# Two loads held back, a clock filler moved, an earlier gather and later landing times in the planned orders of a recommendation-model kernel

## What is computed

```
sparse_embed = emb_tables[field_idx[None, :], x_sparse]
gram = jnp.einsum('bik,bjk->bij', sparse_embed, sparse_embed)
inner = gram[:, iu, ju]
dnn_in = jnp.concatenate([x_dense, z, inner], axis=-1)
h = jax.nn.relu(dnn_in @ w1 + b1)
out = jax.nn.sigmoid(h @ w2 + b2)
```

## Time and profile before

| what | value |
|---|---|
| median of 3 runs | 213.66 us (212.72 to 214.28) |
| profiled execution, its own time | 214.66 us |
| its span, first to last instruction | 212.5 us |
| TensorE busy | 201.6 us (95%) |
| VectorE, ScalarE, GpSimd busy | 148.6, 129.3, 129.4 us |
| mean granted TensorE clock | 0.992 of full speed |

### The profile page before, as it was taken

How to read it: one execution, slowest core, us unless ns; L and a number is a source line. 1 busy time by engine, 2 the same in 40 slices (tenths; PEclk the granted TensorE clock), 3 DMA queues, 4 the chain that set the end, 5 groups by cost and what they waited for, 6 DMA issues and landing times.

```text
span 212.5 us, 3900 instructions
## 1 busy us (share of the span) xinstructions
PE 201.6 (95%) x1340; PEld 161.4 (76%) x1340; DVE 148.6 (70%) x347; ACT 129.3 (61%) x256; POOL 129.4 (61%) x210
## 2 busy tenths in 40 slices
PE   8859999999999999999999799799999999999994
PEld 8834888877777878776887688588888877788882
DVE  3559457488937779879459796777587679773483
ACT  2657443479948939977338844679698558542201
POOL 4887888888787878218877878788788500000000
PEclk9997999999999999999999999999999999999999
DMA  5676999968484912326965667698975637223100
GB/s 153 188 226 201 305 327 344 323 203 281 119 291 125 299 51 63 86 56 169 325 217 178 196 180 189 185 329 299 325 213 161 207 98 212 87 35 63 32 0 0
DMA packets 15388, 39.00 MB, mean 184 GB/s; under 512 B 3881, under 2 KB 5281, under 8 KB 15369
## 3 DMA queue, kind: packets, MB, share of 16 engines
q1 hardware_dynamic: 11688, 35.27, 51.3%
q0 software_dynamic: 3328, 3.41, 7.6%
q10 hardware_dynamic: 353, 0.08, 0.2%
HBM read 37.71 MB, written 0.69 MB: 181 GB/s over the span
## 4 chain that ended last, share of the span: by engine, by line
PE 69%; POOL 15%; DMA 6%; issue 5%; DVE 3%; ACT 2%; DVEq 0%; POOLq 0%; ACTq 0%
PE slot L1079 20%; PE slot L1082 19%; PE slot L1085 19%; POOL E L823 13%; DMA E<-emb,row_idx 5%; PE slot L1039 4%; PE slot L1018 3%; POOL pace L831 2%; DVE G L977 2%; PE slot L1071 1%; PE slot L1069 1%; PE slot L1070 1%; ACT w_hi L847 1%; DMA x_idx<-idx 1%; DVE slot L1003 1%
## 5 line engine op out<-in xcount | busy, mean ns | idle before, releaser
L823 POOL DMA_INDIRECT E<-emb,row_idx x104 | 111.7, 1074 | 37.8 <-POOL pace L831 25.7
L929 DVE TENSOR_TENSOR w_lo<-w_raw,w_hi 128x500 fp32r<-128x500 f32 (+6 forms) x128 | 80.8, 671 | 13.2 <-ACT w_hi L847 12.5
L847 ACT CAST w_hi<-w_raw 128x1000 fp32r<-128x1000 f32 (+6 forms) x64 | 65.7, 1029 | 27.3 <-DMA w_raw<-w 15.4
L1079 PE MATMUL slot<-w_hi,x_hi 128*128 128x500 f32 (+5 forms) x236 | 75.0, 399 | 3.4 <-ACT x_hi L873 2.1
L1082 PE MATMUL slot<-w_lo,x_hi 128*128 128x500 f32 (+5 forms) x236 | 73.3, 390 | 2.3 <-DVE w_lo L929 2.2
L1085 PE MATMUL slot<-w_hi,x_lo 128*128 128x500 f32 (+5 forms) x236 | 72.7, 389 | 0.0
L1079 PEld LDWEIGHTS slot<-w_hi,x_hi 128*128 128x128 f32 (+2 forms) x236 | 43.0, 189 | 15.3 <-ACT x_hi L873 5.0
L1082 PEld LDWEIGHTS slot<-w_lo,x_hi 128*128 128x128 f32 (+2 forms) x236 | 44.5, 189 | 12.1 <-DVE w_lo L929 3.0
L1085 PEld LDWEIGHTS slot<-w_hi,x_lo 128*128 128x128 f32 (+2 forms) x236 | 44.4, 189 | 9.3 <-DVE x_lo L959 0.2
L878 ACT COPY ET<-T 32x128 f32<-32x128 f32 (+4 forms) x88 | 32.1, 364 | 2.0
L946 DVE STREAM_TRANSPOSE T<-E 128x256 f32<-128x256 f32 x24 | 10.6, 443 | 18.8 <-DMA E<-emb,row_idx 18.6
(11 more groups left out here) (39 smaller groups left out, 85.8 us busy)
## 6 DMA issues: line engine op xcount, KB each, us to landing
w_raw<-w SPq DMA_DIRECT2D x32, 501.0 KB, 4.7
w_raw<-w SPq DMA_DIRECT2D x32, 500.0 KB, 4.7
E<-emb,row_idx POOLq DMA_INDIRECT x104, 4.3
w_all<-w SPq DMA_DIRECT2D x1, 1001.0 KB, 6.9
gram_dram<-G SPq DMA_DIRECT2D x8, 84.5 KB
x_in<-gram_dram SPq DMA_DIRECT2D x8, 42.0 KB
x_in<-G SPq DMA_DIRECT2D x4, 58.5 KB
x_in<-G SPq DMA_DIRECT2D x4, 19.5 KB
```

What stands on the lines that cost most here:

```text
L823: nc.gpsimd.indirect_dma_start(out=E[:, k % ER, j, :], out_offset=None, in_=emb_rows, in_offset=bass.IndirectOffsetOnAxis(ap=row_idx[:, at ...
L847: nc.scalar.copy(w_parts(m)[0], w_source(m)).then_inc(w_hi_ready, 1)
L929: nc.vector.tensor_tensor(lo[:, cols], w_source(m)[:, cols], hi[:, cols].bitcast(F32), ALU.subtract)\
L1079: nc.tensor.matmul(acc[q], xh, hi[:, cols[q]], start=first, stop=False)
```

## The change

Four edits. (1) Loads 2 and 3 wait for arrival 1 instead of arrival 0. (2) The five filler matmuls stand ahead of product 3 instead of product 2, and write to the accumulator of the product that follows them. (3) Arrival 16 waits for two gram rounds, and arrival 17 for four. (4) The planner takes landings as 1.5, 2.0, 1.9, 1.9 us for arrivals 0 to 3 and 3.1 us for all later ones, and knows the new waits; all four lists of orders come out of it anew.

```diff
-KEEP_AT, KEEP = 2, 5
+KEEP_AT, KEEP = 3, 5
-PAUSE, RESUME = 16, 4
+HELD_BACK = {16: 2, 17: 4}
+LAND = (1.5, 2.0, 1.9, 1.9, 3.1)
@@ make_orders, gather
-            if k == PAUSE:
-                if ("gram", RESUME - 1) not in done:
+            if k in HELD_BACK:
+                if ("gram", HELD_BACK[k] - 1) not in done:
                     return
-                pool_at = max(pool_at, done["gram", RESUME - 1] + HOP)
+                pool_at = max(pool_at, done["gram", HELD_BACK[k] - 1] + HOP)
             for _ in range(GROUP_GATHERS[ARRIVALS[k][1]]):
                 pool_at += 1.25 if k < 2 else 1.50
                 g_issued.append(pool_at)
-            e_landed.append(pool_at + (1.3 if k < 2 else 1.9))
+            e_landed.append(pool_at + LAND[min(k, len(LAND) - 1)])
@@ make_orders, update
                 if m < BEHIND:
-                    at = e_landed[0]
+                    at = e_landed[1]
@@ build, sync
                     if EARLY <= m < BEHIND:
-                        sp.wait_ge(e_landed[0], 16 * GROUP_GATHERS[ARRIVALS[0][1]])
+                        sp.wait_ge(e_landed[1], 16 * GROUP_GATHERS[ARRIVALS[1][1]])
@@ build, gpsimd
-                if k == PAUSE:
-                    pool.wait_ge(gram_done, RESUME)
+                if k in HELD_BACK:
+                    pool.wait_ge(gram_done, HELD_BACK[k])
@@ build, tensor
-                        nc.tensor.matmul(slot[SLOT[1, 1, "all"]][:, 0:BANK].rearrange("p (a b) -> p a b", a=4), ones[:],
+                        nc.tensor.matmul(slot[SLOT[cell_at(step)]][:, 0:BANK].rearrange("p (a b) -> p a b", a=4), ones[:],
```

## The result

The changed kernel takes 211.81 us in the median of 22 runs, the kernel before 213.65 us in as many beside it. The ratio is 0.9917 with a 95% interval of 0.9895 to 0.9938: 1.8 us, between 1.3 and 2.2, are gained. 211.0 was forecast. A ratio leaves out each kernel's slow runs, those more than 1.5% above its fastest one, so it can differ a little from the ratio of the medians, which are of all runs. The profiled execution took 211.75 us, with a span of 209.4 us where the kernel before had 212.5. These two spans lie 3.1 us apart, more than the medians: the profile before had its clock fall at the start, and it lies 1.0 us above its median.

The account below looks back on a forecast made before the run. TensorE, 95% busy, was taken as the bound, in phase A together with POOL's chain of gathers. Terms -0.15 - 1.42 - 1.09 - 0.35 + 0.3 = -2.7 us took the median from 213.66 to 211.0 us; range 209.2 to 214.6.

Parts of the forecast that it names:

- Start: Loads 2 and 3 and filler: TensorE 3.7 us ahead at product 4, lead mostly lost to later gathers; valued at 0.15 us.
- The predicted 19.6 for product 4: Product 4 starts at 19.6 instead of 23.37, when x_hi of arrival 2 ends.
- What swallows it: Phase A: arrival 4's landing lets 2.5 us of lead pass; gathers at 1.39 us and more apiece wear it off.
- the 62 that was said to be fixed: Product 32, first to need arrival 9's x_hi, was to start again at 62; well before 61.5 would show otherwise.
- Arrival 16: Its gathers go out from 87, everything behind arrival 17 comes 6.3 us earlier; phase B stalls go, less a small cost.
- the 1.42 us: TensorE's idle time ahead of product 78, behind arrival 21's landing, goes: -1.42 us.
- the 0.35 us: Product 66's loss on a low split in VectorE's queue goes: -0.35 us.
- the 1.09 us: TensorE's idle time at 118.27, product 67 waiting for x_hi of (bt 3, group 6), goes: -1.09 us.
- The 0.3 us for the store and fetch: Cost of four gathers flying during the first store and fetch, which feeds inner products: 0.3 us, between 0 and 1.5.
- The orders: New lists from later planned landings: taken as 0; bounds 0.5 us gain and 1.4 us loss per misplaced x_hi.
- Rival D: ScalarE's list, arrivals 4 to 27: x_hi behind a w_hi waiting for TensorE's release of a piece; 216.6 us; chance 0.12.
- Rival C: Phase B stalls only exchanged as new lists place x24 or x_hi elsewhere; 0.5 us left, 213.2 us; chance 0.28.

Follow-up runs that it names:

- filler8: The changed kernel with eight filler matmuls instead of five: 211.51 us, 0.9889 of the kernel before.
- no_filler: The changed kernel without the five filler matmuls: 211.89 us, 0.9928 of the kernel before.
- start_only: The kernel before with only loads 2 and 3 waiting for arrival 1 and the filler ahead of product 3, old lists: 0.9997 of the kernel before.
- no_pace: The changed kernel with POOL's pacing memset and wait only up to the twelfth gather, so denser gathers: 210.45 us, 0.9819 of the kernel before.
- swap_one: The changed kernel with x_hi of (bt 3, group 6) moved ahead of piece 38's w_hi in ScalarE's list: 212.54 us, 0.9879 of the kernel before.
- g16_start: The kernel before with the change's POOL waits, load waits and filler place, old lists with two entries moved: 211.05 us, 0.9877 of the kernel before.
- g16_nopace: The kernel before with the change's POOL waits and pacing only up to the twelfth gather, old lists: 209.69 us, 0.9837 of the kernel before.

## Why the prediction was right, and where it was off

**Start.** Right where it counts. The predicted 19.6 for product 4 was 19.4, the filler's 4.3 was 4.45, the landing of 3.0 was 3.1. The 19.6 was in part luck: it was to be the end of the x_hi of arrival 2, but that was written from 17.86, and TensorE reached product 4 without waiting, at the end of its own work. That the lead would be lost was predicted with 0.15 us left; 0.36 is left at 98.42 in the pair of profiles, and two experiments moved product 4 by 2.2 us one way (filler8) and 1.0 us the other (no_filler) and the end by less than 1 us. That product 1 passes without a stop whatever VectorE's order held in start_only too. Wrong without the new lists was the sentence behind it, that x_hi of arrival 1 is ready by about 11.9: in start_only ScalarE's list put it behind a w_hi that waited for load 2, and it came at 14.64. I had looked at VectorE's list alone.

**What swallows it.** I named the pace of POOL's gathers. The runs bear this out in part only. That TensorE stands still for the landings of arrivals 4 and 5 is shown, and so is that arrival 4, issued 0.7 us earlier, did not land earlier. Product 32 started at 61.51, half a microsecond before the 62 that was said to be fixed. With denser gathers (no_pace) no landing from arrival 6 to 16 was waited for, and the inner products began no earlier than in the changed kernel; so the pace is not all that holds this stretch, and what does is not separated. Beside this: the Trainium skill (DMA: Bandwidth & Descriptors, Anatomy of one DMA) gives a DMA that GpSimd issues 2.0 us plus its bytes at 436 GB/s, an estimated 2.1 us for a gather. The traces do not agree: the gathers issued between 20 and 31 us in the changed kernel took 5.2 us in the median, and the quickest of the whole run 2.4.

**Arrival 16.** The term was -1.42 - 1.09 - 0.35 + 0.3 = -2.56 us. In the pair of profiles phase B gave 2.7 us, which is the sum but not the terms: the 1.42 us and the 0.35 us went as said, the 1.09 us only shrank to 0.68, since the new list of ScalarE puts x_hi behind a w_hi that waits for its load; swap_one, where x_hi stands ahead, has no stop there. Alone on the old lists the edit was worth 1.9% (1.5 to 2.4), 4 us, so I sized it too small; its profile is 3.6 us shorter from the inner products to the end. Of these, 0.9 us are matmuls that take less time, where I had counted 0.35. The 0.3 us for the store and fetch did not appear: the wait at 98.42 is 0.40 us as before.

**The orders.** I took 0 with bounds of -0.5 and of 1.4 us for each misplaced entry. Timed together, the changed kernel and g16_start, which has the other three edits on the old lists with two entries moved, lie 0.1% apart, which is that 0. But edit (3) alone gained 0.8 to 1.1% more than the whole change, by ratios from different groups: about 2 us are lost somewhere in the other three edits. That the sum came to 2.7 us where 1.8 were measured is therefore luck in part: a term that I had too small, and a loss that I did not have at all. Only a part of the loss is placed. The 0.68 us at product 67 belong to the new list of ScalarE; g16_start, on old lists, has a higher ratio than edit (3) alone too, and its profile stands still for 1.93 us ahead of product 12 and 0.90 us at 50.11. Which of the start and the lists costs how much stays open.

My reason, that 3.1 us is nearer to the measured landing and so can be no worse, does not hold as a rule: with the new waits a plan with 3.1 was better than one with 1.9 by 1.3%, with the old waits it was worse by 1.8%. Rival D's mechanism (an x_hi behind a w_hi that waits) is real, but the w_hi waited for its load, not for a release by TensorE. Rival C's place was right (product 67), and it was within 1% as C has it; I had its chance at 0.28. The 0.68 us that were left there are not the whole difference, though.

## What to carry to other kernels

A list of orders written by a planner is tuned to the waits that it was planned with, and the effects of lists and waits are not a sum: here the new waits on the old lists gave 1.9%, a plan with later landings and the old waits lost 1.8%, and the lists of the changed kernel lost 2.7% when one wait was put back. Test a change of waits on the old lists first, and when a stall survives, look in the in-order list at what stands ahead of the late instruction and whether it needs any of it.

A lead made early is worth little if a later chain sets its own times. Adding useless work at the start is a cheap test of that.

A difference of a microsecond in one stretch can't be read from two single profiles: here landings and starts moved by that much between executions of the same instructions.

## What the runs showed of the hardware

The length of an idle time did not tell whether TensorE's clock would fall behind it. After 3.47 us ahead of product 4 (no_filler), 2.01 us in product 1 (g16_nopace) and 1.93 us ahead of product 12 (g16_start) the granted clock stayed at 1.00. After 2.75 us (no_filler), 2.40 us (swap_one) and 1.90 us (no_pace), all ahead of product 12, it came down to 0.50 to 0.54, its lower level, in the windows of the next four microseconds. Such a fall at the start made the filler take 6.15 us instead of 4.45, 1.7 us more.

Two loads of 0.5 MB under way delayed a small gather. The last gather of arrival 1 took 2.8 to 3.1 us to its turn in the ten profiles in which loads 2 and 3 waited for it, and 4.1 to 5.4 us in the four in which they did not.

The landing of a gather scatters from execution to execution. The last gather of arrival 4 took 4.9 us in the changed kernel (25.12 to 29.98), 5.2 us in its second profile and 6.4 us in swap_one (25.21 to 31.58), with the same instructions up to there; issued 0.7 us earlier (no_pace) it took 6.6 us (24.38 to 30.99).
